# Second cross attention: the maxima's queries are spread over the heads by GpSimd, mostly ahead of the loop, in place of VectorE

## The reference

```python
qh = (q @ Wq + bq).reshape(B, LQ, HEADS, D_K).transpose(0, 2, 1, 3)    # B 8, LQ 56, HEADS 16, D_K 8
kh = (k @ Wk + bk).reshape(B, LKV, HEADS, D_K).transpose(0, 2, 1, 3)   # LKV 1500
vh = (v @ Wv + bv).reshape(B, LKV, HEADS, D_K).transpose(0, 2, 1, 3)
scores = jnp.einsum('bhqd,bhkd->bhqk', qh, kh) * scale
attn = jax.nn.softmax(scores, axis=-1)
out = jnp.einsum('bhqk,bhkd->bhqd', attn, vh)
return concat @ Wo + bo                                                # concat: out with heads merged
```

## Time and profile before

| | |
|---|---|
| median of three runs | 625.9 us (622.54 to 626.59) |
| the profiled execution | 630.82 us, its span 629.0 us |
| PE matmul busy | 571.1 us, 91% of the span |
| VectorE busy | 451.6 us, 72% |
| ScalarE busy | 375.3 us, 60% |
| GpSimd busy | 378.8 us, 60% |
| mean granted TensorE clock | 0.975 of full |

### The profile page before, as it was taken

One profiled execution on the slowest core, in us unless ns is written; L12 is line 12 of the kernel. 1 busy time (PEld: TensorE's weight loads), 2 busy tenths in 40 slices (PEclk: granted clock), 3 DMA queues, 4 the chain that ended last, 5 costly groups with the idle time before them and its releaser, 6 DMA issues.

```text
span 629.0 us, 18969 instructions
## 1 busy us (share of the span) xinstructions
PE 571.1 (91%) x8256; PEld 417.1 (66%) x8256; DVE 451.6 (72%) x696; ACT 375.3 (60%) x633; POOL 378.8 (60%) x263
## 2 busy tenths in 40 slices
PE   9688899899999999999989888979898898899897
PEld 4466776557667667666777565656676676677765
DVE  3776836697887787877445774778989988985543
ACT  2145664657667577576462606477787787787452
POOL 1571452389889889864712050167988988979400
PEclk9779999999999999999989999999999999999898
DMA  4730015001101011010004100413432432430000
GB/s 169 216 154 2 4 40 169 11 3 41 27 15 40 2 40 40 3 40 2 3 1 156 26 1 1 101 22 81 103 78 39 91 78 49 81 78 3 2 1 15
DMA packets 33838, 31.81 MB, mean 51 GB/s; under 512 B 27124, under 2 KB 27380, under 8 KB 33756
## 3 DMA queue, kind: packets, MB, share of 16 engines
q1 hardware_dynamic: 33756, 30.60, 18.9%
HBM read 13.06 MB, written 0.23 MB: 21 GB/s over the span
## 4 chain that ended last, share of the span: by engine, by line
PE 47%; POOL 20%; issue 13%; DVE 11%; ACT 8%; DMA 1%; POOLq 0%; DVEq 0%; ACTq 0%
POOL scratch L1293 16%; PE psum L1143 9%; PE psum L1067 5%; PE psum L217 3%; PE psum L1119 3%; DVE scratch L1308 3%; PE psum L1112 2%; PE psum L1114 2%; POOL tok L1402 2%; ACT scratch L1278 2%; PE psum L248 2%; POOL scratch L652 1%; PE psum L1051 1%; PE psum L253 1%; PE psum L363 1%
## 5 line engine op out<-in xcount | busy, mean ns | idle before, releaser
L1293 POOL TENSOR_TENSOR scratch<-scratch 125x896 bf16<-125x896 f32 x145 | 246.3, 1710 | 79.5 <-ACT scratch L1278 78.9
L1278 ACT ACTIVATE scratch<-psum 125x896 f32<-125x896 f32 x192 | 173.7, 917 | 86.7 <-PE psum L1143 51.1
L1308 DVE TENSOR_REDUCE scratch<-psum 128x1 f32<-128x500 f32 x336 | 208.0, 670 | 20.1 <-PE psum L1067 9.5
L1112 PE MATMUL psum<-tok_high,scratch 125*128 125x65 bf16 x1344 | 107.0, 194 | 3.2 <-issue 2.7
L1114 PE MATMUL psum<-tok,scratch 125*128 125x64 bf16 x1344 | 106.4, 194 | 0.0
L1112 PEld LDWEIGHTS psum<-tok_high,scratch 125*128 125x128 bf16 x1344 | 94.7, 98 | 13.8 <-ACT scratch L1278 5.9
L1114 PEld LDWEIGHTS psum<-tok,scratch 125*128 125x128 bf16 x1344 | 88.6, 98 | 16.5 <-issue 0.3
L1293 DVE TENSOR_TENSOR scratch<-scratch 125x896 bf16<-125x896 f32 x47 | 70.7, 1505 | 25.4 <-ACT scratch L1278 24.6
L1143 PE MATMUL psum<-scratch 65*128 65x448 bf16 (+1 forms) x384 | 87.3, 352 | 0.0
L1119 PE MATMUL psum<-tok_high,scratch 125*128 125x65 bf16 x1344 | 72.7, 194 | 3.9 <-POOL scratch L1293 2.3
L1541 PE MATMUL psum<-scratch 128*128 128x500 bf16 x168 | 64.4, 383 | 11.0 <-DVE scratch L1308 8.9
(11 more groups left out here) (341 smaller groups left out, 871.0 us busy)
## 6 DMA issues: line engine op xcount, KB each, us to landing
nrm<-scratch SPq DMA_DIRECT2D x64, 96.0 KB, 2.2
nrm<-w_third SPq DMA_DIRECT2D x32, 96.0 KB, 2.2
raw<-ctx_dram SPq DMA_DIRECT2D x4, 672.0 KB
w_third<-fifth_dram SPq DMA_DIRECT2D x3, 595.0 KB, 6.3
w_third<-third_dram SPq DMA_DIRECT2D x2, 844.0 KB, 8.3
w_third<-third_dram SPq DMA_DIRECT2D x2, 843.5 KB, 6.7
w_fourth<-fourth_dram SPq DMA_DIRECT2D x3, 542.5 KB, 5.8
scratch<-scratch SPq DMA_DIRECT2D x8, 192.0 KB, 2.7
```

What stands on the lines that cost most here:

```text
L1112: nc.tensor.matmul(psum[:, sums, 65 * r:65 * r + 65], rows, t1[:, c, :], start=(c == 0 and r == 0), stop=False, skip_group_check=True)
L1278: nc.scalar.activation(CR["p"][0:CP, n % RING, :].rearrange("p (f n) -> p f n", f=2), psum[0:CP, S:S + 2, 0:HALF], ACT.Exp).then_inc(self. ...
L1293: ops.tensor_tensor(CR["pl"][0:CP, n % RING, :], CR["p"][0:CP, n % RING, :], p_high(n % RING), ALU.subtract).then_inc(done, 1)
L1308: nc.vector.tensor_reduce(mxp[:, r, t:t + 1], bank(B, TB), X_AXIS, ALU.max).then_inc(self.aux_freed, 1)
```

## The change

GpSimd makes the spread queries of batches 1 to 7, into a place of their own for each batch (`q_heads`, over the parameters of the part before, no longer needed), with a semaphore of its own (`q_pool`). VectorE makes only those of batch 0. Batches 1 to 5 are spread ahead of the loop, 6 and 7 behind chunk 8 of batches 0 and 1. The large part of the low queries moves from ahead of the loop to chunk 4 of batch 0.

```diff
+        q_heads = params["fourth"][:, 0:HALF * (BATCH - 1)].bitcast(BF16).rearrange("p (b n) -> p b n", b=BATCH - 1)
...
             def tokens_pool(self, pool, b, c):
                 if b == 0 and c in (1, 2):
                     self.split_tokens(pool, 2, c - 1)
+                if b == 0 and c == 4:
+                    pool.wait_ge(self.low_pool, sum(self.low_on_pool(m) for m in range(c + 1)))
+                    low_queries_pool(pool, 1)
+                if b < 2 and c == 8:
+                    self.plain_by(pool, nc.gpsimd, 6 + b, self.q_pool)
...
-            def plain_queries(self, i):
-                return CR["qb", i]
+            def plain_queries(self, b):
+                return q_heads[:, b - 1, :] if b else CR["qb", 0]
...
                     if k == 0:
-                        pe.wait_ge(self.q_max, b + 1)
+                        pe.wait_ge(self.q_pool if b else self.q_max, max(b, 1))
...
-            def plain_dve(self, dve, b):
-
-                dve.wait_ge(q_high, 1 if b < 2 else 2)
-                nc.vector.tensor_tensor(self.plain_queries(b % 2).rearrange("p (h t) -> p h t", h=HEADS),
-                                        q_plain[:, 56 * b:56 * b + 56].unsqueeze(1).to_broadcast([128, HEADS, SEQ]),
-                                        par("x_heads").bitcast(BF16).rearrange("p (h t) -> p h t", h=HEADS), ALU.mult
-                                        ).then_inc(self.q_max, 1)
+            def plain_by(self, eng, ops, b, done):
+
+                eng.wait_ge(q_high, 1 if b < 2 else 2)
+                ops.tensor_tensor(self.plain_queries(b).rearrange("p (h t) -> p h t", h=HEADS),
+                                  q_plain[:, 56 * b:56 * b + 56].unsqueeze(1).to_broadcast([128, HEADS, SEQ]),
+                                  par("x_heads").bitcast(BF16).rearrange("p (h t) -> p h t", h=HEADS), ALU.mult
+                                  ).then_inc(done, 1)
...
             def front_dve_run(self, dve, beside):
...
-                self.plain_dve(dve, 0)
+                self.plain_by(dve, nc.vector, 0, self.q_max)
...
-                self.plain_dve(dve, 1)

             def beside_dve(self, dve, b, c):
-                if c == 5 and b < BATCH - 2:
-                    self.plain_dve(dve, b + 2)
+                pass
...
             cross2.split_tokens(pool, 1, 1)
             pool.wait_ge(cross2.tok_set, 4)
-            for p in PARTS:
-                low_queries_pool(pool, p)
+            low_queries_pool(pool, 0)
+            for b in range(1, 6):
+                cross2.plain_by(pool, nc.gpsimd, b, cross2.q_pool)
             cross2.run_pool(pool)
```

More of the change, by code:

```diff
@@ L1444, in __init__ @@
                 super().__init__(tag, src, None, wv)
-                self.key_high, self.q_block, self.q_max = (sem(f"{tag}_{n}") for n in ("key_high", "q_block", "q_max"))
+                self.key_high, self.q_block, self.q_max, self.q_pool = (
+                    sem(f"{tag}_{n}") for n in ("key_high", "q_block", "q_max", "q_max_pool"))
                 self.turned, self.key_in = ([sem(f"{tag}_{n}{i}") for i in range(2)] for n in ("turned", "key_in"))
@@ L1540, in pe_unit @@
                         pe.wait_ge(self.key_high, 3 * b + t + 1)
-                    mm = nc.tensor.matmul(bank(B, TB), self.plain_queries(i)[:, 128 * r:128 * r + 128],
+                    mm = nc.tensor.matmul(bank(B, TB), self.plain_queries(b)[:, 128 * r:128 * r + 128],
                                           chunks_of(self.keys_high(i))[:, 4 * t:4 * t + 4, 0:CP], start=True, stop=True)
```

## The result

The changed kernel takes 618.75 us (median of 8 runs, 617.55 to 622.82), the one before 626.25 us (8 runs, 622.54 to 627.83). The ratio is 0.9891, 95% interval 0.9865 to 0.9916: 1.1% faster. The profiled execution took 617.55 us, its span 615.8.

The account below looks back on a forecast made before the run. No engine was full, three nearly so; PE's maxima waited for VectorE's reductions queued behind the spreading. Gains of 5.7 + 1.1 + 0.2 + 0 = 7.0 us from the 625.9 us median gave 618.9 us, range 615.4 to 624.0.

Parts of the forecast that it names:

- The main term: Batches 2 to 5: the spreading leaves VectorE's queue, so PE's maxima wait less; 1.42 us each, 5.7 us in all.
- The price on GpSimd: One spreading of 896 columns on GpSimd takes 1.69 us, between 0.6 and 2.5 us.
- Ahead of the loop: Five spreadings fit into GpSimd's gap before its first subtraction; cost 0, with 5.7 us of cover.
- Batch 1: Gains 1.42 us, loses 0.3 to the spreading for batch 7 behind chunk 8; 1.1 us gained, low end 0.
- Batch 0: Low queries behind chunk 4 and a spreading behind chunk 8 delay GpSimd; 0.2 us gained, low end -0.6.
- GpSimd behind it: In batch 3 GpSimd becomes busy without a gap to the batch's end, subtractions ready 0.3 to 0.9 us before use.
- one sign of being wrong: The prediction would be wrong if TensorE's granted clock fell in the loop; no size given.
- Rival A: In the loop, GpSimd is the bound, so its added work makes the kernel 3.6 us slower, 629.5 us; chance 0.05.
- Rival B: PE's wait goes, but GpSimd's subtractions 0.3 us behind bind; only 3.5 us gained, 622.4 us; chance 0.32.
- Rival C: The stall between chunks 6 and 7 goes too, 1.92 us a batch; 9.5 us gained, 616.4 us; chance 0.13.
- Rival D: Other engines fill PE's stalls in the loop at once; 0 to 1.5 us gained, 625 us; chance 0.1.

Follow-up runs that it names:

- tok_short: The changed kernel with GpSimd's token steps of chunk 3 cut to 64 of 384 columns; 614.54 us in one execution, 21.15 us a batch.
- vector_ahead: The kernel before with all spreadings kept on VectorE, those of batches 1 to 7 in a row ahead of the loop; 618.06 us, ratio 0.9899.

## Why the prediction was right

*The main term* was VectorE's instruction in the way of PE's banks: forecast 1.42 us a batch from the comparison of chunks 7 to 9 in batches 3 and 6, measured 1.50, of which 1.42 in those chunks. The steps are shown one by one: PE's wait for L1309 behind the spreading is gone, and with the instruction out of the loop, made by either engine, a batch lasts the same 21.50 us.

*The price on GpSimd*: 1.69 forecast, 1.68 measured (1672 to 1682 ns). *Ahead of the loop*: cover 5.7 forecast, 5.83 measured, cost none; the first exponential comes 18.07 us behind the start of the small low-queries step both before and after. *Batch 1*: 1.1 us forecast, 1.27 measured, as the spreading behind chunk 8 costs 0.24 and not 0.3.

*Batch 0* is where a term was mis-sized. At half clock I had +0.2 us and the runs show 25.73 - 25.50 = +0.23, in part by luck. From chunk 7 to 9 0.69 us is gained (3.59 to 2.90; forecast 0.67), from chunk 9 to the end 0.59 is lost (7.51 to 8.10; forecast 0.4), and 0.13 is gained ahead of chunk 7, where I had nothing. At full clock I had -0.6 as the low end, from VectorE's reductions 0.85 us sooner; the kernel before is 1.35 us quicker there (24.38), and the change loses 1.12. The clock was at half in batch 0 in 6 of 14 profiled executions, so neither level alone is the kernel's time. The sum at half clock is 4 x 1.50 + 1.27 + 0.23 = 7.5, each term at its forecast or above it; at full clock it is 6.15, as batch 0 falls short by more than the other terms exceed. The forecast of 7.0 lies between the two.

*GpSimd behind it* came out nearly as told: in batch 3 it is busy without a gap through six subtractions, to 500.17, but not to the end of the batch, where it waits twice for an exponential (0.57 and 1.01 us). And one sign of being wrong was badly put: a fall of TensorE's clock in the loop. It fell in batch 0 of both profiled executions, before and after, and says nothing about the change.

*Rival A* (the chain of waits is right, GpSimd is the bound) is refuted for steady batches: 21.50 us, GpSimd still waits 6.8 us in five batches. Its mechanism holds in batch 0 (at full clock above all) and at the end of batch 1. *Rival B* (GpSimd binds 0.3 us later) has the right mechanism where GpSimd got work: 0.24 us in batch 1, 0.92 with the work at chunk 5. *Rival C*: the stall ahead of chunk 7 didn't go, for the reason given, and tok_short shows 0.35 of the 0.50 us to be the token steps' doing. *Rival D* (PE's stalls are filled by others at once) is refuted by 1.50 us a batch. The rule of the Trainium skill (GPSIMD Engine Reference, section 4.1, Engine selection), product on VectorE, would have been right ahead of the loop, where VectorE needs 0.57 us and GpSimd 1.68, and both have the room; inside the loop, at the same place behind chunk 5, it cost 1.50 us a batch on VectorE and 0.92 on GpSimd.

A better version is in sight but not shown by time: with everything ahead of the loop the trace gives 1.6 us less in the six batches at full clock when the key transfers are in time, 0.3 us less at half clock, and the timed ratio (0.9901) can't be told from the change's (0.9891).

## What to carry to other kernels

Look for an iteration of the same loop in which the instruction in question is absent; here the spacing of one marker instruction in both gave the gain to 0.1 us a batch (1.42 for 1.50), where the duration of the instruction (1.79) did not. A chain of waits that runs through one engine doesn't make it the bound if that engine also waits regularly for its input; ask how early its results are when they are read. Before work is moved off a busy loop to another engine's queue, look for a gap ahead of the loop. Count every step that is moved along with it: at full clock the low queries, which had room ahead of the loop, cost 1.3 us of the 7.45 that the change would have gained without their move.

## What the runs showed of the hardware

In these traces VectorE and GpSimd excluded each other for whole instructions when VectorE read two tensors of SBUF. On VectorE 56 columns took 1.36 us beside a 1.68 us subtraction of GpSimd and 0.18 us in GpSimd's gap; 896 columns took 1.79 us beside it and 0.57 to 0.62 with GpSimd idle. GpSimd waited in its turn: its subtraction that started beside a running spreading took 2.06 us (kernel before) or 2.20 (vector_ahead) in place of 1.68. VectorE's reductions from PSUM took 0.66 to 0.68 us throughout the loop, beside the same subtractions too. The Trainium skill (GPSIMD Engine Reference, section 8, Key points) names the shared interfaces, and the trace agrees; these rows show besides that the wait lasted until the other's instruction had ended.

GpSimd's product of two bf16 tensors of 896 columns took 1.68 us, the same as its fp32 by bf16 subtraction of that length.

TensorE's granted clock fell from full (2.4 GHz) to half (1.2 GHz) for 3 to 4 us in batch 0 in 6 of 14 executions, of kernels whose first chunks are much alike; what tips it the runs don't show. It made that batch 1.35 us longer in the kernel before (24.38 to 25.73) and 1.33 with all of GpSimd's additions ahead of the loop (24.10 to 25.43), and not at all in the changed kernel, where GpSimd's queue is full (25.50 at both).
